# Normalising the context rows of a decoder block in two fused VectorE steps, in their working slots

## The reference

```python
x = x + attn(_layernorm(x), ...)
x = x + xattn(_layernorm(x), ctx, ctx, ...)     # Kn = Vn = layernorm(ctx) * g + b
x = x + ffn(_layernorm(x), ...)

def _layernorm(x, g, b):                        # in xattn, over the 256 columns of a row
    mu = mean(x); var = mean((x - mu) ** 2)
    return (x - mu) * rsqrt(var + EPS) * g + b
k = split_heads(Kn @ wk)                        # 16 heads of 64
kn = k / sqrt(sum(k ** 2))                      # per row and head
attn = qn @ kn.T;  out = attn @ v               # no softmax
```

## Time and profile before

| | |
|---|---|
| median of 3 runs | 3776.91 us (3773.48 to 3779.86) |
| the profiled execution | 3773.72 us |
| its span from first to last instruction | 3771.9 us |
| busy in the span: PE, DVE, POOL, ACT | 2734.7, 2013.8, 1341.1, 1201.5 us |
| mean granted TensorE clock | 0.890 |

### The profile page before, as it was taken

The page is one execution under the profiler, slowest core; times in us unless marked ns, Lnnn a source line. Parts: engine busy times, 40 slices in busy tenths (PEclk is TensorE's granted clock), DMA queues, the critical chain, the costliest instruction groups (busy, mean ns, idle before and its releaser), DMA issues.

```text
span 3771.9 us, 49275 instructions
## 1 busy us (share of the span) xinstructions
PE 2734.7 (73%) x14836; PEld 1838.1 (49%) x14884; DVE 2013.8 (53%) x3897; ACT 1201.5 (32%) x1925; POOL 1341.1 (36%) x1020
## 2 busy tenths in 40 slices
PE   0487777877777776777768777687776877778776
PEld 0255544554445544455445545355544555445544
DVE  6546464463745537545465554555455464644637
ACT  1226222271233512234122432225222261222611
POOL 2372224622355122631237222371223712246222
PEclk9999988998799987999879999799888998889987
DMA  6365004650056400573016620364104650046500
GB/s 190 32 125 131 19 6 52 119 142 6 5 73 131 105 6 10 87 131 85 6 20 104 134 56 6 33 131 123 27 6 45 126 132 11 8 55 117 140 6 6
DMA packets 503878, 258.94 MB, mean 69 GB/s; under 512 B 213166, under 2 KB 501702, under 8 KB 502598
## 3 DMA queue, kind: packets, MB, share of 16 engines
q1 hardware_dynamic: 436982, 221.53, 30.0%
q10 hardware_dynamic: 66560, 33.56, 4.2%
HBM read 129.67 MB, written 125.35 MB: 68 GB/s over the span
## 4 chain that ended last, share of the span: by engine, by line
PE 39%; DVE 18%; POOL 13%; issue 11%; ACT 7%; DMA 6%; SPq 1%; ACTq 1%; DVEq 1%; POOLq 0%; another core or an unknown queue 0%
PE PS L1290 33%; PE PS L1293 7%; POOL rn L367 4%; DMA bias_scr<-M 3%; DMA arena<-in_ctx 3%; POOL arena L676 3%; POOL M L701 3%; DVE arena L422 3%; ACT arena L884 2%; ACT arena L891 2%; DVE arena L427 2%; POOL rstd L367 2%; DVE arena L419 2%; POOL arena L439 1%; SPq L540 1%
## 5 line engine op out<-in xcount | busy, mean ns | idle before, releaser
L1293 PE MATMUL PS<-ident,arena 128*128 128x128 f32 (+1 forms) x3356 | 586.5, 305 | 660.2 <-POOL arena L439 285.0
L1293 PEld LDWEIGHTS PS<-ident,arena 128*128 128x128 f32 (+1 forms) x3356 | 416.5, 154 | 871.3 <-POOL arena L439 308.9
L1290 PE MATMUL PS<-arena 128*17 128x128 f32 (+5 forms) x6624 | 738.5, 319 | 130.0 <-ACT arena L891 60.2
L1290 PEld LDWEIGHTS PS<-arena 128*17 128x17 f32 (+2 forms) x6656 | 520.8, 127 | 234.4 <-ACT arena L891 68.3
L367 POOL TENSOR_TENSOR rn<-rn,mhalf 128x16 f32<-128x16 f32 (+1 forms) x136 | 395.8, 2912 | 254.6 <-DVE rn L1230 212.0
L1290 PE MATMUL PS<-cwk,arena 128*128 128x512 f32 (+1 forms) x832 | 376.3, 595 | 25.5 <-ACT arena L823 22.8
L1132 DVE CUSTOM_DVE_ANT_0 PS<-PS,arena 128x512 f32<-128x512 f32 x512 | 342.7, 710 | 95.0 <-PE PS L1290 69.3
L884 ACT ACTIVATE arena<-PS,nmax 128x512 f32<-128x512 f32 x512 | 352.0, 690 | 74.7 <-DVE nmax L1132 64.5
L738 POOL TENSOR_TENSOR arena<-arena,mass_mask 128x512 f32<-128x512 f32 x128 | 163.4, 1277 | 570.3 <-ACT arena L884 570.3
L367 POOL TENSOR_TENSOR rstd<-rstd,mhalf 128x1 f32<-128x1 f32 (+3 forms) x153 | 102.1, 668 | 737.7 <-DVE rstd L380 301.1
L1080 DVE TENSOR_REDUCE ss<-arena 128x16 f32<-128x1024 f32 (+1 forms) x104 | 126.8, 1219 | 300.9 <-ACT arena L829 300.8
(11 more groups left out here) (164 smaller groups left out, 3999.0 us busy)
## 6 DMA issues: line engine op xcount, KB each, us to landing
arena<-bias_scr SPq DMA_DIRECT2D x128, 336.0 KB, 3.2
prob_scr<-arena SPq DMA_DIRECT2D x128, 336.0 KB, 3.8
bias_scr<-M ACTq DMA_DIRECT2D x64, 512.0 KB, 6.2
q_scr<-arena SPq DMA_DIRECT2D x128, 128.0 KB
arena<-k_scr SPq DMA_DIRECT2D x64, 256.0 KB, 10.6
arena<-q_scr SPq DMA_DIRECT2D x128, 128.0 KB, 3.1
arena<-in_ctx SPq DMA_DIRECT2D x96, 128.0 KB, 2.1
arena<-far_scr SPq DMA_DIRECT2D x64, 182.0 KB, 17.2
```

Of the source, the lines that this page charges most:

```text
L1290: return pe.matmul(o, l, r, start=start, stop=stop, **kw)
L1293: return pe.transpose(o, i, ident[0:i.shape[0], 0:i.shape[0]])
```

## The change

The landing buffers are gone. A transfer lands in the slot `Kn[q]`, q = i mod 4, and the whole norm is done there in place. GpSimd keeps only the root. The two steps on DVE are, first, (x - mean) * g, which does not need the root and is issued without waiting for it, and then (that) * rstd + b. Four loads are issued at the start of the stage instead of two and then one. The load of tile i now waits for the g_ctx of tile i - 4, which is the last reader of the slot, and in SP's order the store of keys or queries of a round stands ahead of that round's load.

```diff
-        cin, Kn = carve(512, (2, E)), carve(1024, (4, E))
+        Kn = carve(1024, (4, E), only_attn + 1536)
...
                 def load_ctx(i, q):
-                    n, p = crows(i), q % 2
-                    sp.wait_ge(caff_ready, cdone(b, i - 2) + 1)
+                    n = crows(i)
+                    sp.wait_ge(cg_done, cdone(b, i - 4) + 1)
                     sp.sem_inc(waits_alone, 1)
-                    sp.dma_start(cin[0:n, p, :], d["ctx"][ds(b, 1), ds(i * 128, n), :].rearrange("o p e -> (o p) e"))\
-                        .then_inc(ctx_loaded[p], 16)
+                    sp.dma_start(Kn[0:n, q, :], d["ctx"][ds(b, 1), ds(i * 128, n), :].rearrange("o p e -> (o p) e"))\
+                        .then_inc(ctx_loaded[q], 16)
...
-                load_ctx(0, 0)
-                load_ctx(1, 1)
-                load_ctx(2, 2)
+                for q in range(4):
+                    load_ctx(q, q)
...
                 def more_ctx(i, q):
-                    if exists(i + 3):
-                        load_ctx(i + 3, q + 3)
-                    if 1 <= i <= PARTS:
-                        store_keys(i - 1)
...
+                    if i < PARTS:
+                        store_keys(i)
...
+                    if exists(i + 4):
+                        load_ctx(i + 4, q)
...
-                def affine(i, q):
+                def ctx_root(i, q):
                     n, p = crows(i), q % 2
-                    st = Steps(pool_affine, "pool_affine", b * CT + i)
                     root(pool, rstd[0:n, p:p + 1], c_var, c_rstd, b * CT + i + 1)
-                    pool.wait_ge(cz_ready, cdone(b, i) + 1)
-                    pool.sem_inc(waits_alone, 1)
-                    pool.wait_ge(cg_done, cdone(b, i - 4) + 1)
-                    pool.sem_inc(waits_alone, 1)
-                    st(pool.tensor_tensor(Kn[0:n, q, :], cin[0:n, p, :], rows[0:n, V_G1, :], ALU.mult))
-                    pool.wait_ge(st.sem, st.all())
-                    pool.sem_inc(waits_alone, 1)
-                    pool.tensor_tensor(Kn[0:n, q, :], Kn[0:n, q, :], rows[0:n, V_B1, :], ALU.add)\
-                        .then_inc(caff_ready, cinc(i))
-                    st.close()
...
-                def norm_apply(i, p):
-                    n = crows(i)
-                    x = cin[0:n, p, :]
+                def norm_apply(i, q):
+                    n, p = crows(i), q % 2
+                    x = Kn[0:n, q, :]
+                    dve.scalar_tensor_tensor(x, x, mv[0:n, p, 0:1], rows[0:n, V_G1, :], ALU.subtract, ALU.mult)\
+                        .then_inc(cz_ready, cinc(i))
                     dve.wait_ge(c_rstd, b * CT + i + 2)
-                    dve.tensor_scalar(x, x, mv[0:n, p, 0:1], rstd[0:n, p:p + 1], ALU.subtract, ALU.mult)\
-                        .then_inc(cz_ready, cinc(i))
+                    dve.sem_inc(waits_alone, 1)
+                    dve.wait_ge(cz_ready, cdone(b, i) + 1)
+                    dve.sem_inc(waits_alone, 1)
+                    dve.scalar_tensor_tensor(x, x, rstd[0:n, p:p + 1], rows[0:n, V_B1, :], ALU.mult, ALU.add)\
+                        .then_inc(caff_ready, cinc(i))
```

More of the change, by code:

```diff
@@ L252, in build @@
         bias_stored = sem("bias_stored")
-        ctx_loaded = [sem("ctx_loaded0"), sem("ctx_loaded1")]
+        ctx_loaded = [sem(f"ctx_loaded{q}") for q in range(4)]
         cz_ready = sem("cz_ready", 5)
@@ L705, in norm_root @@
                     root(pool, rn[0:crows(i), q % 2, :], c_norm, c_rnorm, b * CT + i + 1)
-                affine(2, 2)
+                ctx_root(2, 2)
                 norm_root(0, 0)
@@ L711, in ctx_pool @@
                     if exists(i + 3):
-                        affine(i + 3, (q + 3) % 4)
+                        ctx_root(i + 3, (q + 3) % 4)
                     if exists(i + 1):
@@ L1029, in _, with norm_stats @@
                     dve.tensor_scalar(QT[:, c, :], bank(4 + c), cols[:, c:c + 1], None, ALU.add).then_inc(qT_ready, 1)
-                def norm_stats(i, p):
-                    n = crows(i)
+                def norm_stats(i, q):
+                    n, p = crows(i), q % 2
                     st = Steps(dve_norm, "dve_norm", b * CT + i)
-                    per = (CT + 1) // 2 if p == 0 else CT // 2
-                    dve.wait_ge(ctx_loaded[p], 16 * per * b + 8 * (i - p) + 17)
-                    st(dve.bn_stats(bnst[0:n, p, :], cin[0:n, p, :]))
+                    per = (CT + 3 - q) // 4
+                    dve.wait_ge(ctx_loaded[q], 16 * per * b + 4 * (i - q) + 17)
+                    st(dve.bn_stats(bnst[0:n, p, :], Kn[0:n, q, :]))
                     dve.wait_ge(st.sem, st.all())
@@ L1058, in _ @@
                 for i in range(2):
-                    norm_stats(i, i % 2)
-                    norm_apply(i, i % 2)
+                    norm_stats(i, i)
+                    norm_apply(i, i)
                 dve.wait_ge(out_stored, 16 * T * b + 1)
@@ L1065, in _ @@
                         .then_inc(r_dve, 1)
-                norm_stats(2, 0)
-                norm_apply(2, 0)
+                norm_stats(2, 2)
+                norm_apply(2, 2)
                 dve.wait_ge(part0_ready, 2 * b + 3)
@@ L1094, in ctx_dve @@
                     if exists(i + 3):
[L1095 removed]
+                        norm_stats(i + 3, (q + 3) % 4)
                     if exists(i + 1):
@@ L1098, in ctx_dve @@
                     if exists(i + 3):
-                        norm_apply(i + 3, (q + 3) % 2)
+                        norm_apply(i + 3, (q + 3) % 4)
                     scale_k(i, q)
```

16 lines of the change are left out of this document (7 added, 9 removed).

## The result

| | before | changed |
|---|---|---|
| median of 4 runs | 3775.77 us (3773.48 to 3779.86) | 3942.38 us (3940.16 to 3948.37) |
| ratio, with 95% interval | 1 | 1.0443 (1.0424 to 1.0461) |
| span of the profiled execution, mean granted clock | 3771.9 us, 0.890 | 3938.4 us, 0.879 |
| the mean g_ctx product (128x256) | 406 ns | 485 ns |

The changed kernel is 167 us slower; 58 had been forecast, and 3942 lies above the range. The profile's page of the changed kernel answers to the earlier trace rows: engine busy times, the chain by engine, and the group of the statistics of the tiles (busy, mean ns, idle before it and what ended that).

What follows compares the result with a forecast made beforehand. No one engine bounded the whole kernel; GpSimd set the context round at 8.33 us. Start -8.7, nine rounds +23.0 and end -7.1 gave +7.2 us per batch element, +58 over eight: 3834 us, range 3797 to 3910.

Steps and rivals of the forecast that it cites:

- The ring: Context stage: tile i+3's load waits for g_ctx(i-1), closing a dependency loop of 10.6 us a round against 8.33, nine rounds.
- PE's waits: Middle rounds: PE waits about 2.3 us for the second fused step and 0.7 for scale_k.
- The landing: Context load from issue to landing in each round: 2.1 us median, with a floor of 2.0.
- the rival of late loads: Context loads take 3.2 us each beside the far-edge stores: +79 us, 3913; chance 0.08.
- The fused steps: DVE's two norm steps: 0.42 us each plus a gap of 0.25, so 0.67 from first to second.
- GpSimd's norm root: Rival: this root holds up DVE's second fused step, +2.5 us a round, 4014 us; chance 0.05.
- The start: Start of the context stage: four early loads remove the 8.04 us wait, g_ctx(0) ends 8.7 us sooner per batch element.
- The end: After g_ctx(9): key loads no longer lie under far-edge stores, 15.7 us instead of 22.8, -7.1 per batch element.
- The TensorE clock falls: Rival: PE, 72% busy with waits, drops to 1.2 GHz; 15.3 us a round, +340, about 4170; chance 0.04.
- The sum: Per batch element -8.7, +23.0 and -7.1 make +7.2 us, +58 over eight, giving 3834 us.
- a sign of being wrong: Timeline check: g_ctx longer than 3.7 us in the middle of the stage would show the prediction wrong.
- a fifth of the time at that level: TensorE at 1.2 GHz for that share of the time: priced at +70 us.

Runs made afterwards that it cites:

- the open form: Changed kernel with six slots, key and query loads held, and two extra GpSimd roots (16 and 14 columns) for tiles 4 to 12: 3816.06 us, ratio 1.0055.
- the two runs off it: Six slots, held key loads, extra GpSimd roots of 16 and 14 columns: 1.0055; kernel before plus a 12-column GpSimd root for tiles 4 to 12: 1.0318.
- the run with both waits filled: Changed kernel with PE multiplying zeros, nine products before t_ctx and two before g_ctx, where it would wait: 3832.48 us, ratio 1.0106.
- the runs with an open ring: Changed kernel with six slots instead of four, 0.9701, with key loads also held, 0.9469; kernel before with only the two fused VectorE steps, 0.9962.
- the run with the other order: Changed kernel on four slots, scale_k before the next tile's statistics, norm root before short root, t_ctx in the middle of g_ctx: 3806.49 us, 1.0041.

## Why the prediction was wrong

- **The ring was right.** 10.6 us forecast; 10.62 from 651.77 to 662.39, and 10.4 to 10.7 wherever the clock was up. PE's waits were forecast at 2.3 and 0.7 and are 2.23 to 2.34 and 0.70. Six slots, which take the ring away, take the round to 7.1.
- **The landing was right**: in batch element 1 the nine loads landed in 2.0 to 2.1 us, so the rival of late loads falls.
- **The fused steps were mis-sized a little**: 0.48 each instead of 0.42, and 0.63 from start to start instead of 0.67. Links off in both directions cancel.
- **GpSimd's norm root does not hold the second fused step**: it starts at 1159.84, 0.36 us after the root's start, and takes 0.48. So that rival falls. The prediction had it against the earlier trace rows, where the VectorE instruction is a TENSOR_SCALAR with one tile from SBUF; the pair itself is shown only here.
- **The start** gave 9.2 us instead of 8.7, confirmed by the run with three early loads (10 us in batch element 1).
- **The end** gave 6.6 us instead of 7.1. The run that holds the key loads in the kernel before shows its cause to be the one named, and gains 37 us of the 8 x 6.6 = 53 by itself.
- **The step that failed** is the paragraph "The TensorE clock falls", chance 0.04. It compared the new PE share, 72%, with 74% in the score stage and took equal shares for equal clocks, though it wrote that the score stage's waits are shorter. The sum therefore has no term for the clock. Here 2.3 and 0.7 us of waiting in 10.6 sufficed: 55 of the 93 whole g_ctx took over 3.8 us, which the prediction had named as a sign of being wrong, and nine rounds took 108.6 instead of 95.4. It priced "a fifth of the time at that level" at +70; in batch element 1 the excess over the ring is 13.2 us, 106 over all eight. Filling the waits took back 127.
- **A part that the paragraph lacked**: g_ctx is itself a link of the ring that I had written down. A rival that makes a link longer has to be put through the ring. At the low level g_ctx takes 6.5 to 6.7 and the next wait is no shorter, where in the open form it shrinks or vanishes. With the same waits at the full clock, the product takes 485 ns on the ring and 424 and 431 ns in the two runs off it.

Without the clock the sum stands. In the run with both waits filled, batch element 1 has a start of 27.0 us instead of 35.15, nine rounds of 95.5 us where 95.4 were forecast, and an end of 16.2 instead of 22.8: +8.3 us, 66 over all eight, against a forecast of 58. The ratio of that run gives less, +40 us (29 to 51). The kernel before was 19 us slower on its chip than on the first, and no run shows which of the two figures is nearer.

The Trainium skill, GPSIMD Engine Reference, section 4.1 (elementwise work belongs on VectorE), that spoke for a gain, holds in the runs with an open ring: rounds of 7.1 instead of 8.33 us, with two steps of 0.48 us on VectorE where GpSimd took 1.44 for the multiply alone. In the changed kernel the late loads hide it.

What stays open: no run showed which length of wait the clock just bears at this load, nor why about half of the rounds with such waits left it up.

## What to carry to other kernels

When buffers are merged, write down who frees the slot and walk from there back to the same instruction; if the sum of that ring is longer than the round of the busiest engine, the merge costs more than a cheaper operation gives, and two more slots may be the whole cure (here 1.0443 became 0.9701, and 0.9469 with the key loads held). Where TensorE is a link of the ring, add its waits up and count its work at the lower clock as well, since a slow stretch there does not shorten the next wait. An order of transfers that is harmless at one round length can collide at another, so look at the end of the stage again after each gain in its middle.

## What the runs showed of the hardware

- The granted clock fell from 2.4 to 1.2 GHz in stretches after waits of 2.2 and 0.7 us in rounds of 10.6, though PE was busy 23.41 of 32.00 us in the window before. The Trainium skill, TensorE: Matmul & The Clock Gate, section "HAM oscillation — how this bites in real kernels", describes an engine that waits for a transfer in every step and is at the low clock after each. The trace agrees that waits which come back in every round bring the clock down; here they are waits for VectorE, shorter than those described there, and the clock was not low after each (8 of 15 fast g_ctx were followed by a slow one). The open form adds that the low stretch can be absorbed by the next wait.
- A far edge on GpSimd (128x1024, two operands in SBUF) held a fused VectorE step that started beside it: 1.82 us instead of 0.48, ending 0.28 us after the far edge. A norm root (128x16, also two operands) did not hold one. The Trainium skill, SBUF — State Buffer, section "Who interferes with whom", has it that a VectorE instruction with two SBUF inputs contends with a GpSimd instruction that reads SBUF. The far edge agrees, the root does not. In the kernel before, a far edge also held the TENSOR_SCALAR of the maximum of tile 12, which has one input tile (L1082 at 2995.38, 1.66 us instead of 0.17).
- The norm root itself takes 2.9 to 3.0 us; started 0.27 us after `scale_k`, in the run with the other order, it took 3.71 (656.39); and an extra root on 16, 14 and 8 columns took 2.90, 2.58 and 1.64.
- A far-edge store landed 16.0 to 19.9 us after its issue beside SP's loads of keys (16.0 and 18.6 in the kernel before, 19.3 with six slots, 19.9 in the changed kernel, where nothing waited for it), and in 4.1 to 4.8 us in the changed kernel's middle rounds.
